# Flamingo block on one core: layer 0's queries, turned chunks and output product in another order, and the feed-forward's first turns reordered

## The reference

```
x = x + tanh(g_xattn[0]) * xattn0(layernorm(x), ctx)      # 16 heads of 16, 77 keys, softmax
x = x + tanh(g_ffn[0])   * moe0(layernorm(x))             # 8 experts, top 2
x = x + tanh(g_xattn[1]) * xattn1(layernorm(x), ctx)      # 16 heads of 64
x = x + tanh(g_ffn[1])   * ffn1(layernorm(x))             # 256 -> 1024 -> 256, activations rounded to 16 bits
# x: (4, 1024, 256) fp32; ctx: (4, 77, 192) fp32
# ffn1: x_q = round(x * 32767 / max|x|) and the same for gelu(hidden); weights in int8 steps
```

## Time and profile before

| | us |
|---|---|
| median of 3 runs | 1161.31 (1160.58 to 1162.45) |
| the profiled execution, its own time | 1163.3 |
| its span in the trace | 1161.2 |
| PE / DVE / ACT / POOL busy | 1057.4 / 916.9 / 834.7 / 539.4 |

### The profile page before, as it was taken

How to read it: one execution, slowest core, us unless ns; L and a number is a source line. 1 busy time by engine, 2 the same in 40 slices (tenths; PEclk the granted TensorE clock), 3 DMA queues, 4 the chain that set the end, 5 groups by cost and what they waited for, 6 DMA issues and landing times.

```text
span 1161.2 us, 26321 instructions
## 1 busy us (share of the span) xinstructions
PE 1057.4 (91%) x8919; PEld 775.3 (67%) x8919; DVE 916.9 (79%) x1960; ACT 834.7 (72%) x2382; POOL 539.4 (46%) x515
## 2 busy tenths in 40 slices
PE   6888888868969999999999999589999999889898
PEld 5666666645537777777777777357777777645477
DVE  5999999957845687666666667479999999789798
ACT  4988889836656456556556667378888888569896
POOL 5888888732252122122122111178889887500140
PEclk9999999979989999999999999889999999989899
DMA  6443334349672343333333335345252423010034
GB/s 150 118 128 110 110 110 133 123 128 284 189 206 61 53 137 90 118 101 121 124 104 120 121 115 161 112 127 161 68 158 67 154 74 92 28 38 0 1 119 137
DMA packets 128814, 132.12 MB, mean 114 GB/s; under 512 B 24792, under 2 KB 112973, under 8 KB 128557
## 3 DMA queue, kind: packets, MB, share of 16 engines
q1 hardware_dynamic: 119901, 112.17, 32.0%
q0 software_dynamic: 6480, 17.70, 5.5%
q10 hardware_dynamic: 2304, 0.59, 0.3%
HBM read 82.78 MB, written 47.64 MB: 112 GB/s over the span
## 4 chain that ended last, share of the span: by engine, by line
PE 57%; DVE 4%; ACT 4%; issue 2%; DMA 1%; POOL 1%; DVEq 0%; SPq 0%; ACTq 0%; POOLq 0%
PE exp_ps_h L1527 15%; PE exp_ps_y L1540 9%; PE a_ps_o L1953 9%; PE a_ps_sc L1937 8%; PE f_ps_h L2264 5%; PE exp_ps_y L1546 5%; PE a_ps_p L1924 3%; ACT exp_h L1590 2%; DVE f_hlo L2395 2%; PE exp_ps_x L1506 1%; PE f_ps L2447 1%; PE f_ps L2443 1%; PE f_ps_x L2255 1%; DVE all_xn L2404 1%; PE a_ps_x L1911 1%
## 5 line engine op out<-in xcount | busy, mean ns | idle before, releaser
L1590 ACT ACTIVATE exp_h<-exp_ps_h,exp_b_now 128x256 f32<-128x256 f32 (+1 forms) x320 | 124.7, 440 | 142.4 <-PE exp_ps_h L1527 142.4
L1491 POOL DMA_INDIRECT exp_xg<-xn,all_token_of x71 | 84.4, 1188 | 304.0 <-PE exp_ps_x L1506 288.5
L1527 PE MATMUL exp_ps_h<-exp_xhi,exp_w_now 128*128 128x256 bf16 (+1 forms) x1280 | 196.4, 263 | 5.9 <-DVE exp_xlo L1625 5.9
L1986 ACT ACTIVATE a_z<-a_ps_sc,a_nmx 128x77 f32<-128x77 f32 x512 | 159.3, 367 | 35.6 <-DVE a_nmx L2088 35.6
L1527 PE MATMUL exp_ps_h<-exp_xlo,exp_w_now 128*128 128x256 bf16 (+1 forms) x640 | 161.4, 263 | 0.0
L1703 DVE TENSOR_TENSOR exp_hlo<-exp_h,exp_hhi 128x512 bf16<-128x512 f32 (+1 forms) x160 | 99.4, 632 | 70.4 <-ACT exp_hhi L1597 68.5
L1540 PE MATMUL exp_ps_y<-moe_w2s,exp_hhi 128*128 x568 | 134.2, 379 | 1.3 <-DVE exp_y L1722 1.3
L1527 PEld LDWEIGHTS exp_ps_h<-exp_xhi,exp_w_now 128*128 128x128 bf16 x1280 | 120.6, 99 | 20.7 <-issue 8.3
L1986 ACT ACTIVATION_READ_ACCUMULATOR a_z<-a_ps_sc,a_nmx 128x1 f32 x512 | 127.0, 248 | 0.0
L1953 PE MATMUL a_ps_o<-a_v_now,a_phi 128*128 128x256 bf16 (+1 forms) x640 | 106.6, 272 | 2.3 <-DVE a_plo L2077 2.3
L1937 PE MATMUL a_ps_sc<-a_k_now,a_xhi 128*128 128x462 bf16 (+1 forms) x384 | 98.6, 341 | 3.4 <-DMA a_k_now<-fold_klo 2.2
(11 more groups left out here) (279 smaller groups left out, 2735.5 us busy)
## 6 DMA issues: line engine op xcount, KB each, us to landing
a_stage<-in_L_ffn_W_dram SPq DMA_DIRECT2D x64, 256.0 KB, 3.2
y_slots<-exp_y SPq DMA_DIRECT2D x71, 128.0 KB, 1.7
fold_k<-route_kst SPq DMA_DIRECT2D x16, 308.0 KB, 4.5
fold_v<-route_vst SPq DMA_DIRECT2D x16, 308.0 KB
exp_job_in<-fold_k SPq DMA_DIRECT2D x14, 352.0 KB, 3.3
exp_job_in<-fold_v SPq DMA_DIRECT2D x14, 352.0 KB, 3.3
a_x<-in_x_dram SPq DMA_DIRECT2D x32, 128.0 KB, 2.3
x<-a_xo SPq DMA_DIRECT2D x32, 128.0 KB, 1.7
```

Source lines behind the costliest of these rows:

```text
L1491: pool.indirect_dma_start(out=xg[:, v, u, :], out_offset=None, in_=xn_dram[:, :], in_offset=bass.IndirectOffsetOnAxis(ap=at.bitcast(U32), ...
L1527: mm = pe.matmul(hidden[:, i, f % 2, slots(j)], w1_now[:, v, k, hl, f * P:(f + 1) * P], xx[:, k, slots(j)], start=(q == 0), stop=(q == len ...
L1590: ins = act.activation(h[:, f, slots(j)], hidden[:, i, f % 2, slots(j)], ACT.Gelu_apprx_tanh, bias=b1_now[:, v, f:f + 1])
L1986: ins = act.activation(z[:, u, h * KEYS:(h + 1) * KEYS], ps_sc[:, j, (h - SB[j][0]) * KEYS:(h - SB[j][0] + 1) * KEYS], ACT.Exp, bias=nmx[: ...
```

## The change

In layer 0's attention:

- TensorE: the queries of tile T+1 move from the head of slot T+1 into slot T, behind the values of chunks 0 to 3 of tile T-2; queries(0) stands ahead of the slots. Scores come first in a slot, then the output product. The third turn of probabilities comes before `turn_x` and the first two after it. The values are done in three parts: chunks 0 to 3, then 4 to 7, then 8 and 9, in the order of `turns` inside each.
- ScalarE: `attnT` moves behind normalisation and `qT`; the third copy moves ahead of the second; both high parts stand together at the slot's end.
- VectorE: the maximum moves ahead of `xo`.
- GpSimd: the low parts of tile T-1 are made in slot T: the first at its head, the second behind the power; then the bias, and last the normalisation.

In the feed-forward the scale is ready after three tiny instructions; its reciprocal and `in_step` (or `out_step`) follow behind the first scaling. In slot 1 TensorE makes two products of group 0 ahead of group 1's transposes. `magic` is set in the first half; in the second, ScalarE and GpSimd wait for the scale itself (count 8) and ScalarE's high parts for `out_step` (count 10).

```diff
+    part = [[i for i in turns if blocks[i][0] // 4 == k] for k in range(3)]
 GpSimd, slot
+                if has(T - 1):
+                    pool.wait_ge(s["hi_done"], 2 * T - 1)
+                    pool.tensor_tensor(w1[:, at, 1, cols], stage[:, v, 0, :], w1[:, at, 0, cols],
+                                       ALU.subtract).then_inc(s["lo_done"], 1)
                 if has(T + 2):
                     power(T + 2, u)
+                if has(T - 1):
+                    pool.wait_ge(s["hi_done"], 2 * T)
+                    pool.tensor_tensor(w2[:, 2 * T - 2:2 * T, D:2 * D], ...
 TensorE, slot
                     mm.then_inc(s["scores_done"], 1)
+                if has(T - 3):
+                    output(T - 3)
                 if has(T - 2):
                     pe.wait_ge(s["norm_done"], T - 1)
...
                     turn_p(T - 2, 2)
                 if has(T + 1):
                     turn_x(T + 1)
                 if has(T - 2):
...
+                    pe.wait_ge(s["pT_done"], 3 * (T - 2) + 1)
+                    attend(T - 2, part[0])
+                    pe.wait_ge(s["pT_done"], 3 * (T - 2) + 2)
+                if has(T + 1):
+                    queries(T + 1)
+                if has(T - 2):
+                    pe.wait_ge(s["pT_done"], 3 * (T - 2) + 3)
+                    attend(T - 2, part[1])
+                    attend(T - 2, part[2]).then_inc(s["pv_done"], 1)
                 if T == 0:
                     pe.wait_ge(weights_in, 16 * N_WEIGHTS)
                     values(0, 1)
 feed-forward, TensorE, step
+                    ahead = 2 if isinstance(g, int) and g == 1 else 0
+                    if ahead:
+                        pe.wait_ge(s["lo_done"], 2)
+                        for f in range(ahead):
+                            product(0, 0, f)
                     if has(g):
                         for p in range(2):
                             pe.wait_ge(s["rounded"], g * 2 + p + 1)
 feed-forward, VectorE
+                scale_of(dve, s["step"], 0, ps_h[:, 1, 0:1], x_scale, tmp)
...
                 integers(0, 0)
+                step_of(dve, s["step"], 0, x_scale, C.wi_step, in_step)
+                dve.memset(magic[:, :], MAGIC).then_inc(s["magic_set"], 1)
```

More of the change, by code:

```diff
@@ L427, in _, with queries, output, attend @@
             pe.wait_ge(keys_in, 16 * 3)
+            def queries(T):
+                pe.wait_ge(s["xnT_done"], T + 1)
+                for g in range(ng):
+                    for k in range(KD):
+                        mm = pe.matmul(ps_q[:, g * P:(g + 1) * P], wq[:, k, g * P:(g + 1) * P], xnT[:, k, :],
+                                       start=(k == 0), stop=(k == KD - 1))
+                mm.then_inc(s["q_done"], 1)
+            def output(T):
+                pe.wait_ge(s["attn_done"], T + 1)
+                for g in range(ng):
+                    mm = pe.matmul(ps_o, attnT[:, g, :], wo[:, g, :], start=(g == 0), stop=(g == ng - 1))
+                mm.then_inc(s["o_done"], 1)
+            def attend(T, some):
+                for i in some:
+                    c, q, half = blocks[i]
+                    j, g = q // ng, q % ng
+                    mine = [cc for cc, qq, _ in blocks if qq == q]
+                    n = min(P, ROWS - c * P)
+                    mm = pe.matmul(ps_v[32 * j:32 * j + 32, g * P:(g + 1) * P], vblk[0:n, T // TPB % 2, c, half, :], pT[0:n, c, :],
+                                   start=(c == mine[0]), stop=(c == mine[-1]))
+                return mm
             keys(0, 1, 0)
@@ L430, in _ @@
             pe.wait_ge(queries_in, 32)
+            queries(0)
             def slot(T, t, b):
                 u = t % 2
[L434 to L445, removed]
                 if has(T):
@@ L469, in slot @@
                 if has(T - 2):
+                    if T == 2:
+                        pe.wait_ge(s["kT_done"], 1)
+                    for j in range(2):
+                        wait(pe, s["pT_done"], 3 * (T - 3) + 2 * j + 1)
+                        turn_p(T - 2, j)
                     wait(pe, s["xo_done"], T - 2)
-                    bv = (T - 2) // TPB
                     if t == 2:
[L473 to L485, removed]
+                        pe.wait_ge(s["v_done"], (T - 2) // TPB + 1)
+                    pe.wait_ge(s["pT_done"], 3 * (T - 2) + 1)
[7 more added lines that the diff above has]
+                    attend(T - 2, part[2]).then_inc(s["pv_done"], 1)
                 if T == 0:
@@ L539, in slot @@
                     ins.then_inc(s["qT_done"], 1)
+                if has(T - 3):
+                    act.wait_ge(s["pv_done"], T - 2)
+                    wait(act, s["o_done"], T - 3)
+                    act.activation(attnT[:, :, :].rearrange("p g t -> p (g t)"), ps_v, ACT.Copy).then_inc(s["attn_done"], 1)
                 if has(T - 1):
@@ L2235, in _ @@
                 largest(1)
[L2236 to L2237 removed]
+                scale_of(dve, s["step"], 5, ps_h[:, 1, 0:1], h_scale, tmp)
+                dve.wait_ge(s["magic_set"], 1)
             @block.tensor
@@ L2259, in step @@
                         pe.wait_ge(s["lo_done"], g * 2)
[L2260 to L2266 removed]
+                        for f in range(ahead, FCH):
+                            product(g - 1, 1 - v, f)
                 largest(0)
```

97 lines of the change are left out of this document (40 added, 57 removed).

## The result

The changed kernel takes 1176.27 us (median of 4 runs, 1173.83 to 1179.62) against 1161.45 (4 runs, 1160.58 to 1162.45): ratio 1.0127, 95% interval 1.0113 to 1.0141. It is slower by 14.8 us, outside the predicted range of 1157.5 to 1172.0. The profiled execution took 1174.15, its span is 1172.2 against 1161.2: +11.0. The other 3.8 are between the executions: the profiled one of after is 2.1 under its median, that of before 1.9 over.

A forecast was written before the change was run, and what follows sets the result against it. Attention was taken as bound by a 6.82 us circle through VectorE's clamp and GpSimd's low part. First tiles +4.9, steady tiles -3.5, end +0.5, feed-forward -1.4 gave +0.5 us: median 1161.8, range 1157.5 to 1172.

The forecast's parts named there:

- parts 1 and 2, nine steps, 0.98: Attention's steady tiles: the last two parts of the values products start their records in nine steps of 0.11, 0.98 us.
- circle copy to values to copy: Attention's steady tiles: loop from ScalarE's copy through values, attnT and relu to the next copy, claimed to set 6.68 a tile.
- rival (a): Attention's values: products held in program order, circle 7.05 a tile, total +10.2 us, 1171.5; chance 0.30.
- change back: TensorE's added tiling switch from full-array queries to column groups, taken at 0.09; the known switch to full array costs 0.21.
- First tiles: Attention's slots 0 to 2: queries ahead of the projection wait for xnT, costing 4.9 us, bounds 3.2 and 5.7.
- the same again: Attention's slot 1: the projection again waits behind xnT and queries; scores 1 to 2 take 9.74 against 7.38, +2.4.
- A circle closes: Attention before: VectorE's clamp is held by GpSimd's low part, closing a loop from z to z of 6.82 us.
- The long slots that I left unchanged: Attention: four of 29 intervals also build a block's key or value tile on VectorE; no saving claimed there.
- End: Attention's end: two transposes go first and the last values parts start behind the last copy, +0.5 us.
- First product at 22.3 on the old axis: Feed-forward's first half: TensorE starts group 0's products at 22.2 instead of 23.74, taking 1.4 us off the end.
- this case and its 0.7: Feed-forward's first half: if the clock stays lower through the transposes, the gelu comes 0.7 later and 0.7 is saved.
- if GpSimd takes the ports first: Feed-forward's second half, costed at 0: GpSimd, released by the same semaphore, going first would cost 1.3 us more.

The follow-up runs named there:

- e_dealt: The changed kernel with the products of chunks 4 to 9 in one list, dealt round the column groups; 1172.21 us, ratio 1.0083 to before.
- e_low: The kernel before with GpSimd's order of the change alone (low parts early, normalisation last); 1158.33 us, ratio 0.9967.
- e_copy3: The kernel before with only the third copy of turned probabilities put ahead of ScalarE's w1 high part; 1169.96 us, ratio 1.0064.
- e_pair: The kernel before with both GpSimd's order of the change and the third copy ahead of the w1 high part; 1146.84 us, ratio 0.9869.
- e_ffn_fix: The kernel before with the change's feed-forward part alone, GpSimd's first scaling waiting for VectorE's first part; 1160.75 us, ratio 0.9986.
- e_f1: The kernel before with e_pair's attention edits and e_ffn_fix's feed-forward, but out_step computed ahead of VectorE's first part; 1148.39 us, ratio 0.9876.

## Why the prediction was wrong

**The step that failed: "parts 1 and 2, nine steps, 0.98".** With the sum's other terms as measured, the circle copy to values to copy is:

| term | predicted | after |
|---|---|---|
| copy, to first product | 0.73 | 0.74 |
| part 0, change to the full array | 1.00 | 0.96 |
| queries, change back | 0.97 | 1.09 |
| parts 1 and 2, to the last record's start | 0.98 | 1.26 |
| last record, semaphore | 0.31 | 0.31 |
| attnT | 0.29 | 0.28 |
| relu to copy | 2.40 | 2.45 |
| sum | 6.68 | 7.09 |

So the circle was the right one, and what rival (a) was about, products held behind others, came true in it. That its 7.05 a tile is so near 7.09 is partly luck: it had the two parts at 1.35 (measured 1.26) and the change back at 0.09 (measured 0.21). Sorted by chunk, the three products on group 3 stand behind seven others, five of them on group 2. e_dealt shows that the order is the cause: dealt out, the term is 1.01. I had named this mechanism and given it 0.30, on the ground that something is passed over in the earlier trace rows.

The records of the single products show what is passed over. They don't name the column group; I infer it, for passes that follow one another on one group are 0.11 to 0.13 us apart, so two that start 7 ns apart stand on different groups. The ten products of after's second stretch go to groups 2,3,2,2,1,2,2,3,3,3. The first passes of the first two start at 125.208 and 125.215, their second passes together at 125.342 and 125.348. The third product (group 2) starts at 125.451, and the fifth (group 1, free) at 125.457, ahead of the fourth (group 2, 125.669). The eighth, the first of the three on group 3, starts at 125.893, 5 ns behind the sixth (125.888) and ahead of the seventh (126.106), although group 3 had started nothing since 125.348. So a product that waits for its own group is passed over, but as soon as a second one waits for the same group, all behind it are held. In e_dealt the product on group 1 passes one waiting on group 2 and one on group 3, and nothing is lost. This reading fits both stretches; no run isolates it. The Trainium skill (TensorE: Matmul & The Clock Gate, Part 3: Packing small matmuls) has matmuls start strictly in program order. This trace agrees in that products are held, but not to the letter: the fifth starts 0.21 ahead of the fourth, and in strict order the term would be about 1.48 (an estimate: 0.90 to the seventh's start and the 0.58 that the last three took), not 1.26.

The second error in the sum is the change back, taken at 0.09: 1.09 less 0.88 is 0.21, the same as the known one. The 0.88 runs from the first query's start to the last one's, so the whole 0.21 had to be added and not its excess over a step; with it the prediction's own sum is 6.80, where it says 6.70. The Trainium skill (TensorEngine Tiling (Array Packing), Tiling Modes) has a change of tiling mode drain the engine; the trace agrees in that both changes cost more than a step of 0.11. This error alone takes 0.12 of the predicted gain of 0.14: e_dealt, with the order mended, still takes 6.84 a tile.

**First tiles: 7.5 (and up to 11.5) for 4.9.** Scores of tile 1 at 22.96 were predicted at 22.9, with half clock in slot 0: right, but with luck in it. The 2.83 taken for the projection is no half-clock time: e_dealt's took 3.62 and its scores of tile 1 came at 23.92. In after the clock record goes to full speed at 20.33, within the projection, and it took 2.82. Slot 1 was priced at full clock, "the same again"; behind the same idle time ahead of the queries TensorE was at half clock there too: from the queries' start to the projection's 1.87 for the 0.9 of the sum, projection 3.40 for 1.90. That is 2.5 of the 2.6 missing: scores of tile 2 came at 35.09 for 32.6. The bound of 5.7 was too low for the same reason.

**What bounded before.** "A circle closes" at the clamp was true but only half of it. e_low, e_copy3 and e_pair show a second circle of 6.81 beside it, through the third copy and the queries. The prediction went on to the circles of the new order, so this cost it nothing; but it is why removing a stall of 0.5 us a tile gave nothing in steady slots. The long slots that I left unchanged became 7.09 like the others.

**End.** +0.5 predicted, +0.9 measured; in e_dealt, with the products dealt out, it is +0.6, so the same mis-sized term accounts for most of the difference.

**Feed-forward.** First product at 22.3 on the old axis: at 1032.62, that is 22.29, 10.33 of it being the shift: right. Its first half gave 0.8, not 1.4. Group 1's transposes still ran at half clock (1.77 us), and the first gelu came 0.5 later in its stretch instead of 0.15; the prediction named this case and its 0.7. The second half was costed at 0 with +1.3 as the bound "if GpSimd takes the ports first"; GpSimd did start first, by 0.14 us, and that cost 1.4. e_ffn_fix shows that it was that: from the second reduction to the last matmul before takes 68.2 us, after 69.6 and e_ffn_fix 68.4.

**The sum.** Predicted +4.9 - 3.5 + 0.5 - 1.4 = +0.5. Measured in the profiled executions: +7.5 + 4.5 + 0.9 - 0.8 + 1.4 = +13.5, less 2.6 in an untouched stretch: 10.9. The tiles' sign came out the other way: 8.0 of the 13 lie there. The forecast's range took (a) and the start's bound one at a time; both came together, with the race on top.

## What to carry to other kernels

When an engine stands back to back because a small instruction stretches, follow what ended just in time on the other engines too: two circles of one length look like one, and only taking both away shows it. Small matmuls on several column groups are to be dealt round the groups in every stretch between two waits, not only in the whole list: two in a row that wait for one busy group held those behind them here. Before moving TensorE's work behind a wait near the start, price everything after the gap at half clock, and where one semaphore releases VectorE and GpSimd, make one wait for the other's end.

## What was unexpected of the hardware

- A start of the same instructions cost 7.5 us in one execution and 11.5 in another, by when the records of TensorE went from the 1.2 GHz level to the 2.4 GHz one (scores of tile 2 0.81 or 1.41, by about 31 or 43 us).
- The granted clock of the windows view read 1.00 over stretches whose records lasted as at half clock (e_dealt's projection 3.62 at 29.10). That trace holds no clock record before 43.42, where one of full speed begins, and the view reads 1.00 where it has none. At the start, durations tell the level more surely than that column.
- Of small fp32 products on four column groups, one waiting on its group was passed over (125.457 ahead of 125.669) and a second one on that group held the rest (group 3 idle until 125.893).
- GpSimd 0.14 us ahead stretched VectorE's 1.28 to 2.48, while its own part took 1.55, as in e_f1 (1.54), where it starts behind VectorE's end. In before VectorE starts 0.19 first: its part takes 1.28 and GpSimd's 1.97. Whoever starts first keeps its time in these traces, and the later one is stretched, VectorE by 1.20 and GpSimd by 0.42.
